# Experts by pairs of tiles with copied gate and up weights, and own places for the first eight tiles

## The chip, the core and the metric

One core of a Trainium2 chip. The metric is the device time of one execution in microseconds; the kernel before took 3332.89 us (median of three executions, 3332.68 to 3335.68).

## What is computed

Two blocks on x of shape (8, 1024, 256), each with a residual and a layer norm, all in f32:

```
x = x + LN(attn(LN(x)));  x = x + LN(ffn(LN(x)))
attn: Q, K, V of rms(x); elu on Q and K; linear attention by heads of 16:
      w = Q1 (K1' V) - lambda * Q2 (K2' V);  two rms norms; gelu MLP with W1, W2
ffn:  rms, rope, causal softmax attention with 16 query and 4 key heads, Wo; h = clip(x + .)
      flat = rms(h); probs = softmax(flat @ Wr); top 2 of 8 experts, weights normalised
      o_e = (silu(flat Wg_e) * (flat Wu_e)) Wd_e;  out = clip(h + sum_e w_e o_e)
```

Wg and Wu are (8, 256, 512), Wd is (8, 512, 256). A token takes part in two of the eight experts.

## The kernel before, in words

The 8192 tokens are 64 tiles of 128 (TT = 64, P = 128). There are three parts, one behind the other.

**`attention_kernel` (L95).** It computes everything up to the routing. Each engine's program is one list in order. A loop over periods p from -2 to 87 and over 24 slots i in each places every operation of every tile: "if i == 6 and have(p + 1): project(p + 1, False)" puts the query and key projection of tile p + 1 at slot 6 of period p. A slot fixes only the order on an engine; what really starts an operation are the waits (`need`). The causal attention ("back") is interleaved from slot 5 of period 12 on (`START`, L317), so that periods -2 to 11 hold only the front, the linear attention and the projections. The steps of the front that matter here: `x_statistics` (VectorE, L1017), `x_coefficients` (GpSimd), `normalized` (ScalarE), `transpose_x` (TensorE, L1363), `x_turned`, `project` (queries and keys into bank GA, L1408; values into bank GB, L1404), `exponentials` and `values` (ScalarE), `elu` (VectorE, L1030), `key_products` in four parts (GpSimd, L560), `sum_heads` in two halves and `turn_sums` (TensorE, L1418, L1427, bank SUM), `query_products` and `query_sums` in four parts each (VectorE, L1043, L1052). `sum_heads` of a tile waits until all four query products of the tile before have read bank SUM. `EARLY` (L320) moves the last tiles' output projection and routing forward in the list. Behind the loop the last four tiles (60 to 63) are projected and routed one by one. SyncE then loads wd, writes the last rows of h2 and writes pad rows behind each expert's rows (L479, L483). VectorE's `plan_tiles` works out the expert and the first row of every tile of the experts part. A normalised row with its routing values is scattered by GpSimd to two places of scratch_xs, sorted by expert (`scatter`, L649). At the end a block clears 123 semaphores, on all engines (L1679 to L1704).

**`run_experts` (L1719).** 136 tiles of 128 rows, in a rolled loop of eight. For each tile: SyncE loads its rows (L1765, four ahead), TensorE transposes them (`turn_x`, L1861), ScalarE evacuates (L1803), TensorE multiplies with XT stationary and the expert's gate and up weights moving, 512 columns (L1870), ScalarE applies silu (L1808), VectorE multiplies gate and up (L1831), TensorE transposes the product (L1897), ScalarE evacuates it (L1819), TensorE multiplies with wd (L1906), VectorE weights the result (L1853), and GpSimd adds it to h2 in memory by an indirect, accumulating DMA (L1790), each one behind the one before. Each f32 matmul is two records in the profile. Before a tile TensorE's sequencer reads the expert's number from memory (`value_load`, L1866). The order on TensorE in step n is:

```
gate(n+1)   transposes of AG(n)   turn_x(n+2)   up(n+1)   down(n)
```

**`finish` (L1912).** 16 groups of four tiles of h2 are loaded, clipped (GpSimd), normalised and added to x (L1937 to L2009).

A `Signal` is a semaphore with the count of its increments.

## Time and profile before

| | |
|---|---|
| median of three executions | 3332.89 us |
| the profiled execution | 3336.61 us, its span 3334.8 us |
| TensorE matmul busy | 2874.7 us (86%) |
| VectorE busy | 2155.8 us (65%) |
| GpSimd busy | 1764.0 us (53%) |
| ScalarE busy | 1671.5 us (50%) |
| mean granted TensorE clock | 0.945 |

The shares are means over stages with different limits, so they say little about one stage. PE is TensorE's matmuls, PEld its weight loads, DVE VectorE, ACT ScalarE, POOL GpSimd, SP SyncE, a q behind a name its sequencer. In a timeline a line has its start in us, its length, the engine, the line of the kernel and the operation; in brackets stands how long the engine was idle before it and what ended that.

### The profile page before, as it was taken

To read this page: it belongs to the slowest core of one execution; us is meant where nothing else is said; L and a number is where in the kernel's file an instruction comes from. 1 tells how busy PE (TensorE), PEld (TensorE's weight loads), DVE (VectorE), ACT (ScalarE), POOL (GpSimd) and SP (SyncE) were. 2 spreads that over 40 slices of the span, in tenths; PEclk is the share of its full clock that TensorE was granted. 3 is DMA by queue.
4 is the path that set the end of the run, shared out by engine and by line. 5 is a ranking of instruction groups with operands and counts; after the bars stand their busy time and mean duration, and the time that the engine had idled before them with its cause. 6 is when DMAs were issued, how large, how long until landed. Compare 5 with 4: busy or idle time off the path is not lost. (4 is left out here: it accounts for less than half of the span.)

```text
span 3334.8 us, 54048 instructions
## 1 busy us (share of the span) xinstructions
PE 2874.7 (86%) x17348; PEld 1708.5 (51%) x17349; DVE 2155.8 (65%) x4620; ACT 1671.5 (50%) x3836; POOL 1764.0 (53%) x2330
## 2 busy tenths in 40 slices
PE   3567899889989989988998997988869999999990
PEld 3344545555555555554554554444336666666660
DVE  3566887888888798789889878757522222222226
ACT  1234657657656666766765765765512222222224
POOL 5686755765775775676676576232132222222225
PEclk8777999999999999999999999999979999999995
DMA  1000000000000000000000000001243333333325
GB/s 46 0 10 10 11 9 13 14 25 13 27 20 16 29 19 19 19 22 24 12 27 22 14 25 17 14 26 58 85 125 55 58 59 57 51 59 57 57 46 205
DMA packets 102670, 123.21 MB, mean 37 GB/s; under 512 B 14384, under 2 KB 90160, under 8 KB 102448
## 3 DMA queue, kind: packets, MB, share of 16 engines
q1 hardware_dynamic: 76720, 85.54, 8.5%
q0 software_dynamic: 25728, 34.88, 6.1%
q8 instruction: 118, 1.93, 0.2%
q14 instruction: 104, 0.85, 0.1%
HBM read 58.23 MB, written 61.36 MB: 36 GB/s over the span
## 5 line engine op out<-in xcount | busy, mean ns | idle before, releaser
L897 ACT ACTIVATE wd<-SP_ 128x512 f32<-128x512 f32 (+3 forms) x1536 | 723.5, 488 | 474.1 <-PE SP_ L1576 334.4
L1194 DVE TENSOR_REDUCE NM<-MX 128x1 f32<-128x512 f32 (+3 forms) x1216 | 762.4, 654 | 244.4 <-PE MX L1533 148.3
L1530 PE MATMUL MX<-KST,QST 96*128 96x512 bf16 (+3 forms) x1536 | 454.7, 334 | 102.7 <-DVE NM L1194 91.1
L560 POOL TENSOR_TENSOR wg<-wu 128x1024 f32<-128x1024 f32 x256 | 487.7, 1925 | 103.8 <-DVE wu L1030 103.6
L1573 PE MATMUL SP_<-QST,KST 99*128 99x512 bf16 (+3 forms) x1536 | 501.7, 333 | 33.6 <-ACT wd L897 16.1
L1790 POOL DMA_INDIRECT scratch_h<-Y,XG x136 | 211.4, 1554 | 601.5 <-DVE Y L1853 504.0
L1831 DVE TENSOR_TENSOR AG<-UB,SL 128x512 f32<-128x512 f32 x136 | 94.1, 692 | 469.3 <-PE UB L1870 469.3
L1808 ACT ACTIVATE SL<-GB 128x512 f32<-128x512 f32 x136 | 81.3, 598 | 603.7 <-PE GB L1870 603.7
L1043 DVE TENSOR_TENSOR wg<-wu,SUM 128x1024 f32<-128x1024 f32 x256 | 310.2, 1212 | 101.2 <-PE SUM L1427 101.2
L1530 PEld LDWEIGHTS MX<-KST,QST 96*128 96x128 bf16 x1536 | 135.1, 98 | 431.5 <-DVE NM L1194 301.3
L1590 PE MATMUL OA<-wd,V 128*32 128x512 f32 (+3 forms) x3072 | 331.9, 504 | 0.9 <-ACT wd L897 0.4
L1052 DVE TENSOR_REDUCE wu<-wg 128x64 f32<-128x1024 f32 x256 | 307.0, 1203 | 0.3
L1418 PE MATMUL SUM<-ident,wg 128*128 128x128 f32 x2048 | 274.6, 294 | 15.1 <-DVE BR L1172 11.5
L1418 PEld LDWEIGHTS SUM<-ident,wg 128*128 128x128 f32 x2048 | 257.2, 154 | 23.8 <-DVE BR L1172 14.6
L1870 PE MATMUL GB<-wg,XTm 128*128 x544 | 258.1, 597 | 0.3 <-issue 0.3
L1906 PE MATMUL DN<-wd,AGT 128*128 x1088 | 257.1, 379 | 0.8 <-ACT AGT L1819 0.8
L1870 PE MATMUL UB<-wu,XTm 128*128 x544 | 256.8, 594 | 0.0
L1906 PEld LDWEIGHTS DN<-wd,AGT 128*128 128x128 f32 x1088 | 206.6, 190 | 86.6 <-issue 65.6
L1573 PEld LDWEIGHTS SP_<-QST,KST 99*128 99x128 bf16 x1536 | 153.7, 100 | 175.1 <-ACT wd L897 96.9
L1576 PE MATMUL SP_<-mask_kq,identb 128*128 128x128 bf16 x1024 | 224.2, 222 | 0.0
L576 POOL TENSOR_TENSOR R<-R,powers 128x16 f32<-128x16 f32 x64 | 187.1, 2924 | 5.3
L1533 PE MATMUL MX<-mask_qk,identb 128*128 128x128 bf16 (+2 forms) x704 | 174.8, 248 | 0.0
(246 smaller groups left out, 5001.3 us busy)
## 6 DMA issues: line engine op xcount, KB each, us to landing
XG<-scratch_xs SPq DMA_DIRECT2D x136, 130.0 KB, 2.1
wu<-in_L_attn_x SPq DMA_DIRECT2D x64, 128.0 KB, 2.1
scratch_x<-wu SPq DMA_DIRECT2D x64, 128.0 KB, 1.7
scratch_h<-H SPq DMA_DIRECT2D x64, 128.0 KB, 1.7
X<-scratch_x SPq DMA_DIRECT2D x16, 512.0 KB, 3.9
out<-X SPq DMA_DIRECT2D x16, 512.0 KB, 2.9
wg<-in_L_ffn_Wg SPq DMA_DIRECT2D x8, 512.0 KB, 4.3
wu<-in_L_ffn_Wu SPq DMA_DIRECT2D x8, 512.0 KB, 4.7
```

What stands on the lines that cost most here:

```text
L560: sg["prod1"].by(pool.tensor_tensor(P1[:, k // 2, (k % 2) * hh * D:(k % 2 + 1) * hh * D].rearrange("p (h e d) -> p h e d", h=hh, e=HD), QK ...
L897: sg["exp"].by(act.activation(PR[:, n % 8, q0:512], SP_[:, n % 2, q0:512], ACT.Exp))
L1043: sg["prod2"].by(dve.tensor_tensor(products(k), QK[:, t % 2, r].rearrange("p (h e) -> p h e", e=HD).unsqueeze(2).broadcast_to(shape), KVP. ...
L1052: sg["attn"].by(dve.tensor_reduce(AT[:, t % RAT, r].rearrange("p (h d) -> p h d", d=HD), products(k), AX.X, ALU.add))
L1194: sg["mx"].by(dve.tensor_reduce(NM[:, u % 2, part, i, h:h + heads], MX[:, index % 2, 0:heads * n].rearrange("p (h n) -> p h n", n=n), AX.X ...
L1418: m = pe.matmul(SUM[:, c * P:(c + 1) * P], P1[:, half, h * D + c * P:h * D + (c + 1) * P], ident[:, :], is_transpose=True, start=half == 0 ...
L1530: m = pe.matmul(out[:, k], QST[0:MROW, j % 2, g * G + h + k, i * P:(i + 1) * P], KST[0:MROW, keys % RK, g, 0:n], start=k == 0, stop=not la ...
L1573: m = pe.matmul(SP_[:, n % 2, q0:512], KST[0:KROWS, keys % RK, g, (kt % CH) * P:(kt % CH + 1) * P], QST[0:KROWS, j % 2, g * G + h, q0:512] ...
L1576: m = pe.matmul(SP_[:, n % 2, q0:q0 + P], identb[:, :], mask_kq[:, :], start=False, stop=True)
L1590: m = pe.matmul(OA[32 * h:32 * (h + 1), q0:512], V1[:, keys % RV, kt % CH, g, :], PR[:, (G * k + h) % 8, q0:512], start=kt == 0, stop=last ...
L1870: m = pe.matmul(out[:, s % 2], XT[:, s % 2, c * P:(c + 1) * P], w[:, bass.ds(e, 1), c, :].squeeze(1), start=c == 0, stop=c == FC - 1)
L1906: m = pe.matmul(DN[:, 0:D], AGT[:, s % 2, c * P:(c + 1) * P], wd[:, bass.ds(e, 1), c, :].squeeze(1), start=c == 0, stop=c == FK - 1)
```

## The change

- The experts part works on pairs of tiles, 256 rows at a time. Each expert's rows are padded to a multiple of 256, and there are 71 pairs. Now the gate and up weights are stationary and 256 columns of XT are moving, so that the product comes out transposed and its transposes (L1897) and their evacuation fall away. The stationary gate weights are first copied by ScalarE from the expert's place into a buffer WG of two (`gate_weights`), the up weights by VectorE into WU (`up_weights`). Both engines read the expert's number themselves. TX has one buffer. The loop has four pairs in a body and seven pairs behind it.
- The order on TensorE in step n is gate(n+1), down(n), up(n+1), turn_x(n+2). On ScalarE it is silu(n+1), x_evac(n+2), gate_weights(n+2). On VectorE it is the weighting of n, gate(n+1), up_weights(n+2). GpSimd scatters each pair in two halves.
- In the fill, tiles 0 to 7 have places of their own (`filled`, with the number of slots by which a step comes sooner than its old slot as the last argument). In the drain `EARLY` is 12 slots a tile instead of 6. SyncE loads six of wd's eight parts before the last rows of h2.
- Pads have 256 rows; four go through SyncE's queue and four through ScalarE's. The semaphores of the first part aren't cleared, and later parts count on from their values (`past`).
- `finish` loads two groups of four tiles with one DMA.

```
+PAIR = 2 * P
+REGION = B * S + PAIR
+
+
+UNROLL = 4
+NPAIRS = TT + E - 1
...
-        EARLY = 0, 6, 14
+        EARLY = 0, 12, 14
...
+        FILL = 8
+
+        def filled(p, i, age, slot, sooner):
+
+            return [t for t in range(p - age - 2, p - age + 4) if 0 <= t < TT
+                    and (t + age) * SLOTS + slot - (sooner if t < FILL else 0) == p * SLOTS + i]
...
+                need("h2a", LAST_CHUNK)
+                load_weight(wd, "Wd", range(1, 3))
+                need("pv", NSTEPS)
+                load_weight(wd, "Wd", range(3, 7))
                 for t in range(LAST_CHUNK, TT):
                     need("h2", t + 1)
                     sg["h2out%d" % (t % 2)].by(sp.dma_start(h2d[:, t, :], H2[:, t % 2]), 16)
-                need("pv", NSTEPS)
-                load_weight(wd, "Wd", range(3, 7))
                 need("h2a", TT)
-                load_weight(wd, "Wd", range(3))
+                load_weight(wd, "Wd", range(1))
                 need("lg", TT)
                 load_weight(wd, "Wd", range(7, E))
                 need("tables", 3)
-                sp.dma_start(dram["xs"][E * REGION:E * REGION + P], pad[:, :]).then_inc(padded, 16)
+                sp.dma_start(dram["xs"][E * REGION:E * REGION + PAIR].rearrange("(j p) f -> p j f", p=P), pads).then_inc(padded, 16)
                 need("ends", 1)
-                for e in range(E):
+                for e in range(E // 2):
...
+                    sp.dma_start(dram["xs"][bass.ds(at, PAIR), :].rearrange("(j p) f -> p j f", p=P), pads).then_inc(padded, 16)
...
-                        if i == 10 and have(p + 1):
-                            key_products(p + 1, 0)
-                        if i == 12 and have(p + 1):
-                            key_products(p + 1, 1)
-                        if i == 12 and have(p + 1):
-                            key_products(p + 1, 2)
+                        for t in filled(p, i, -1, 10, 4):
+                            key_products(t, 0)
+                        for t in filled(p, i, -1, 12, 5):
+                            key_products(t, 1)
+                        for t in filled(p, i, -1, 12, 4):
+                            key_products(t, 2)
...
-                        if i == 19 and have(p + 2):
-                            x_coefficients(p + 2)
+                        for t in filled(p, i, -2, 19, 14):
+                            x_coefficients(t)
...
+                        for t in filled(p, i, -1, 6, 6):
+                            exponentials(t)
...
+                        for t in filled(p, i, -2, 18, 11):
+                            normalized(t)
...
+                for e in range(E // 2, E):
+                    at = act.value_load(endi[0:1, e:e + 1], min_val=0, max_val=E * REGION)
+                    act.dma_start(dram["xs"][bass.ds(at, PAIR), :].rearrange("(j p) f -> p j f", p=P), pads).then_inc(padded, 16)
...
+                        for t in filled(p, i, 0, 3, 1):
+                            query_products(t, 0)
...
+                        for t in filled(p, i, -1, 9, 6):
+                            elu(t)
+                        for t in filled(p, i, 0, 9, -4):
+                            query_products(t, 2)
...
+                        for t in filled(p, i, 0, 15, 2):
+                            query_products(t, 3)
...
+                        for t in filled(p, i, 0, 0, -1):
+                            sum_heads(t, 0)
...
+                        for t in filled(p, i, -1, 6, 6):
+                            project(t, False)
+                        for t in filled(p, i, -1, 8, 5):
+                            project(t, True)
...
+                        for t in filled(p, i, -2, 20, 5):
+                            transpose_x(t)
...
-        every = [x.sem for x in sg.all] + [x.sem for x in setup.all] + loaded + stored
-        with nc.Block() as clearing:
-
-            @clearing.sync
-            def _(sp):
-                for s in every[0::5]:
-                    sp.sem_clear(s)
...
+        XG = sb("XG", [P, U, 2, ROW])
+        XT = sb("XTm", [P, 2, FC, PAIR])
+        WG = sb("WG", [P, 2, FC, F])
+        WU = sb("WU", [P, 2, FC, F])
+        SL = sb("SL", [P, 2, 2 * PAIR])
+        AG = sb("AG", [P, FK, PAIR])
+        Y = sb("Y", [P, 2, 2, D])
+        picks = sb("picks", [P, U, 2])
+        share = sb("share", [P, U, 2])
+        GB = ps("GB", [P, 2, 2 * PAIR])
+        UB = ps("UB", [P, 2, 2 * PAIR])
+        TX = ps("TX", [P, FC, PAIR])
+        DN = ps("DN", [P, 2, D])
...
+                for s in range(count):
+                    for j in range(2):
+                        pool.wait_ge(sg["y"].sem, 2 * (n0 + s) + j + 1 + CREDIT)
+                        if not (first and s == 0 and j == 0):
+                            pool.wait_ge(sg["added"].sem, (2 * (n0 + s) + j) * 16)
+                            pool.sem_inc(sg["freed"].sem, 1)
+                        pool.indirect_dma_start(
+                            out=dram["h2"], out_offset=bass.IndirectOffsetOnAxis(ap=XG[:, s % U, j, ROW - 1:ROW].bitcast(U32), axis=0),
+                            in_=Y[:, s % 2, j], in_offset=None, compute_op=ALU.add).then_inc(sg["added"].sem, 16)
...
+                act.activation(XT[:, s % 2], TX[:, :, :], ACT.Copy).then_inc(sg["xT"].sem, 1)
...
+            def silu(n):
+                for b in range(2):
+                    act.wait_ge(sg["g"].sem, 2 * n + b + 1)
+                    act.wait_ge(sg["ag"].sem, 2 * n + b - 1 + CREDIT)
+                    act.activation(SL[:, b], GB[:, b], ACT.Silu).then_inc(sg["silu"].sem, 1)
+
+            def expert(n):
+                at = texpi[0:1, n:n + 1] if isinstance(n, int) else texpi[0:1, bass.ds(n, 1)]
+                return act.value_load(at, min_val=0, max_val=E - 1)
+
+            def gate_weights(s, n):
+                e = expert(n)
+                act.activation(WG[:, s % 2], wg[:, bass.ds(e, 1)].squeeze(1), ACT.Copy).then_inc(sg["wg"].sem, 1)
+
+            act.wait_ge(wsem, 16 * 3 * E)
+            gate_weights(0, 0)
             x_evac(0, 0)
+            gate_weights(1, 1)
             x_evac(1, 1)
-            silu(0, 0)
-
-            def body(n0, i, last):
-                for s in range(U):
-                    if not (last and s + 1 >= U):
-                        silu(s + 1, n0 + s + 1)
-                    act.wait_ge(sg["tpa"].sem, n0 + s + 1 + CREDIT)
-                    act.activation(AGT[:, s % 2], TA[:, :], ACT.Copy).then_inc(sg["agT"].sem, 1)
-                    if not (last and s + 2 >= U):
+            silu(0)
+
+            def body(n0, i, count, last):
+                for s in range(count):
+                    if not (last and s + 1 >= count):
+                        silu(n0 + s + 1)
+                    if not (last and s + 2 >= count):
                         x_evac(s, n0 + s + 2)
-            act.sem_inc(sg["agT"].sem, CREDIT)
+                        gate_weights(s, n0 + s + 2)
...
+            def gate(n):
+                dve.wait_ge(sg["down"].sem, n + CREDIT)
+                for b in range(2):
+                    dve.wait_ge(sg["u"].sem, 2 * n + b + 1)
+                    dve.wait_ge(sg["silu"].sem, 2 * n + b + 1)
+                    dve.tensor_tensor(AG[:, 2 * b:2 * b + 2].rearrange("p k t -> p (k t)"), UB[:, b], SL[:, b], ALU.mult)\
+                        .then_inc(sg["ag"].sem, 1)
...
+                dve.tensor_copy(WU[:, s % 2], wu[:, bass.ds(e, 1)].squeeze(1)).then_inc(sg["wu"].sem, 1)
...
+                    for j in range(2):
+                        dve.tensor_scalar(Y[:, s % 2, j], DN[:, j], share[:, slot, j:j + 1], None, ALU.mult).then_inc(sg["y"].sem, 1)
+                    if not (last and s + 1 >= count):
+                        gate(n + 1)
+                    if not (last and s + 2 >= count):
+                        up_weights(s, n + 2)
...
+            def project(s, n, w, out, ready, done):
+                pe.wait_ge(sg[ready].sem, n + 1)
+                for b in range(2):
+                    pe.wait_ge(sg["ag"].sem, 2 * n + b - 1 + CREDIT)
+                    for k in range(2):
+                        f = 2 * b + k
+                        for c in range(FC):
+                            m = pe.matmul(out[:, b, k * PAIR:(k + 1) * PAIR], w[:, s % 2, c, f * P:(f + 1) * P],
+                                          XT[:, s % 2, c], start=c == 0, stop=c == FC - 1)
+                    m.then_inc(sg[done].sem, 1)
...
+            def combine(n, e):
+                pe.wait_ge(sg["ag"].sem, 2 * n + 2 + CREDIT)
+                pe.wait_ge(sg["y"].sem, 2 * n + CREDIT)
+                for j in range(2):
+                    for f in range(FK):
+                        m = pe.matmul(DN[:, j], AG[:, f, j * P:(j + 1) * P], wd[:, bass.ds(e, 1), f, :].squeeze(1),
+                                      start=f == 0, stop=f == FK - 1)
+                m.then_inc(sg["down"].sem, 1)
...
+            def body(n0, i, count, last):
+                for s in range(count):
                     n = n0 + s
-                    more = not (last and s + 1 >= U)
-                    e = e1
+                    more = not (last and s + 1 >= count)
+                    e = expert(n)
                     if more:
-                        e1 = expert(n + 1)
                         pe.wait_ge(sg["xT"].sem, n + 2)
-                        pe.wait_ge(sg["ag"].sem, n + CREDIT)
-                        project(s + 1, n + 1, e1, wg, GB, "g")
-                    pe.wait_ge(sg["ag"].sem, n + 1 + CREDIT)
-                    pe.wait_ge(sg["agT"].sem, n + CREDIT)
-                    for c in range(FK):
-                        m = pe.transpose(TA[:, c * P:(c + 1) * P], AG[:, s % 2, c * P:(c + 1) * P], identm[:, :])
-                    m.then_inc(sg["tpa"].sem, 1)
-                    if not (last and s + 2 >= U):
+                        project(s + 1, n + 1, WG, GB, "wg", "g")
+                    combine(n, e)
+                    if more:
+                        project(s + 1, n + 1, WU, UB, "wu", "u")
+                    if not (last and s + 2 >= count):
                         turn_x(s + 2, i)
...
+            for n in range(0, NB, 2):
+                two = halves[n // PER][:, n % PER:n % PER + 2].rearrange("p n u f -> p (n u) f")
+                sg[f"loaded{n // 2}"].by(sp.dma_start(two, hd[:, n * U:(n + 2) * U, :]), 16)
```

Some thirty further lines of the slot tables change from "if i == a and have(p + b)" to `filled` in the same way, `context` on VectorE waits for its own earlier step ("ctx"), and `plan_tiles` shifts by 8 bits instead of 7.

## Rows read from the trace of the kernel before

**Rows 1.** Windows: start:end, length, busy us of five engines; clock, DMA, GB/s.
```profile
25.00:191.00 166.00, 87.85 (x390) 67.35 (x390) 81.31 (x99) 35.57 (x85) 102.24 (x99) 0.74 0.00 1
191.00:307.00 116.00, 79.39 (x381) 58.55 (x380) 73.67 (x109) 51.16 (x111) 98.92 (x138) 0.76 0.04 12
307.00:2404.00 2097.00, 1887.55 (x13502) 1069.66 (x13502) 1723.43 (x3547) 1352.68 (x3131) 1270.42 (x1846) 0.98 0.07 23
...
2458.00:3256.00 798.00, 795.84 (x2992) 496.05 (x2992) 194.83 (x544) 186.81 (x409) 209.82 (x135) 1.00 0.32 55
```

**Rows 2.** Timeline of TensorE over one tile of the experts: start us, length, instructions.
```profile
3003.95 0.60 PE L1897 MATMUL TA<-ident,AG 128*128 128x128 f32 x4
3004.39 0.38 PE L1861 MATMUL TX<-ident,XG 128*128 128x128 f32 x2
...
3006.32 1.89 PE L1906 MATMUL DN<-wd,AGT 128*128 x8
3008.05 1.88 PE L1870 MATMUL GB<-wg,XTm 128*128 x4
3009.77 0.27 PE L1897 MATMUL TA<-ident,AG 128*128 128x128 f32 x1
```

**Rows 3.** Timeline of the last two tiles of the experts, all engines.
```profile
3252.33 0.60 PE L1897 MATMUL TA<-ident,AG 128*128 128x128 f32 x4
...
3252.97 0.60 ACT L1819 ACTIVATE AGT<-TA 128x512 f32<-128x512 f32 x1 [3.23 <-PE TA L1897]
...
3253.69 1.97 PE L1906 MATMUL DN<-wd,AGT 128*128 x8 [0.76 <-ACT AGT L1819]
3253.88 1.55 POOL L1790 DMA_INDIRECT scratch_h<-Y,XG  x1 [4.05 <-DVE Y L1853]
3255.70 0.48 DVE L1853 TENSOR_SCALAR Y<-DN,share 128x256 f32<-128x256 f32 x1 [2.31 <-PE DN L1906]
3258.23 1.55 POOL L1790 DMA_INDIRECT scratch_h<-Y,XG  x1 [2.80 <-DMA scratch_h<-Y,XG]
```

**Rows 4.** Single tile and lines, whole run: count, ns min/median/max, first, last.
```profile
L1906 PEld LDWEIGHTS DN<-wd,AGT x1088: 187/190/190, 2470.2 to 3255.1; 128*128 128x128 f32 x182
...
L1866 PEldq TENSOR_LOAD <-texpi x153: 299/496/776, 2459.5 to 3244.4; - x153
L1866 PEldq SEQ_ASSERT  x153: 18/18/18, 2460.2 to 3245.2; - x153
...
L752 ACT ACTIVATE wu<-wu x64: 621/622/630, 32.2 to 2026.2; 128x512 f32<-128x512 f32 x64
...
L769 ACT ACTIVATE SQ<-wu x64: 399/407/427, 61.5 to 2077.9; 128x256 f32<-128x256 f32 x64
```

**Rows 5.** Timeline of TensorE and of VectorE in the fill.
```profile
47.83 0.71 PE L1427 MATMUL SUM<-turn,wg 128*128 128x128 f32 x4 [0.47 <-ACT wg L758]
...
101.47 6.42 PE L1418 MATMUL SUM<-ident,wg 128*128 128x128 f32 x32
...
212.81 0.71 PE L1427 MATMUL SUM<-turn,wg 128*128 128x128 f32 x4
...
109.11 1.22 DVE L1043 TENSOR_TENSOR wg<-wu,SUM 128x1024 f32<-128x1024 f32 x1 [6.25 <-PE SUM L1427]
...
116.95 1.21 DVE L1043 TENSOR_TENSOR wg<-wu,SUM 128x1024 f32<-128x1024 f32 x1
```

**Rows 6.** Clearing block on TensorE; timeline of VectorE at the seam, GpSimd after.
```profile
L1704 PEldq EVENT_SEMAPHORE_RANGE_CLEAR  x24: 56/56/63, 2451.8 to 2454.5; - x24
...
2405.97 0.42 DVE L1236 TENSOR_TENSOR CTX<-MX,RC 128x256 f32<-128x256 f32 x1
...
2407.79 0.30 DVE L1132 MAX8 top<-LG 128x8 f32<-128x8 f32 x3
...
3267.91 1.04 POOL L1951 TENSOR_SCALAR wg<-wg 128x1024 f32<-128x1024 f32 x1 [8.12 <-DMA wg<-scratch_h]
3269.40 1.04 POOL L1951 TENSOR_SCALAR wg<-wg 128x1024 f32<-128x1024 f32 x1 [0.45 <-DMA wg<-scratch_h]
```

More of the change, by code:

```diff
@@ L66, with __init__, past @@
 class Signal:
-    def __init__(self, sem):
+    def __init__(self, sem, n=0):
         self.sem = sem
-        self.n = 0
+        self.n = n
+        self.before = n
+    def past(self, k):
+        return self.before + k
     def by(self, instruction, k=1):
@@ L1833, in _, with expert, up_weights @@
+            def expert(n):
+                at = texpi[0:1, n:n + 1] if isinstance(n, int) else texpi[0:1, bass.ds(n, 1)]
+                return dve.value_load(at, min_val=0, max_val=E - 1)
+            def up_weights(s, n):
+                e = expert(n)
+                dve.tensor_copy(WU[:, s % 2], wu[:, bass.ds(e, 1)].squeeze(1)).then_inc(sg["wu"].sem, 1)
             dve.sem_inc(sg["ag"].sem, CREDIT)
             dve.sem_inc(sg["y"].sem, CREDIT)
-            gate(0, 0)
-            def body(n0, i, last):
-                for s in range(U):
+            dve.wait_ge(wsem, 16 * 3 * E)
@@ L1844, in body @@
-                    dve.tensor_scalar(share[:, s, 0:1], first_choice, here, gain, ALU.is_equal, ALU.mult)\
-                        .then_inc(sg["picked"].sem, 1)
-                    if not (last and s + 1 >= U):
-                        gate(s + 1, n + 1)
-                    dve.wait_ge(sg["picked"].sem, n + 1)
-                    dve.tensor_tensor(share[:, s, 1:2], share[:, s, 0:1], second, ALU.add).then_inc(sg["share"].sem, 1)
-                    dve.wait_ge(sg["down"].sem, n + 1)
-                    dve.wait_ge(sg["share"].sem, n + 1)
@@ L1904, in body @@
-                    pe.wait_ge(sg["y"].sem, n + CREDIT)
-                    for c in range(FK):
-                        m = pe.matmul(DN[:, 0:D], AGT[:, s % 2, c * P:(c + 1) * P], wd[:, bass.ds(e, 1), c, :].squeeze(1),
-                                      start=c == 0, stop=c == FK - 1)
-                    m.then_inc(sg["down"].sem, 1)
+                        project(s + 1, n + 1, WG, GB, "wg", "g")
+                    combine(n, e)
+                    if more:
+                        project(s + 1, n + 1, WU, UB, "wu", "u")
@@ L1968, in norm @@
             def norm(n):
[L1969 removed]
+                act.wait_ge(sg["shift"].sem, sg["shift"].past(n + 1))
                 for u in range(U):
```

371 lines of the change are left out of this document (155 added, 216 removed).

## The prediction

> **What bounds the kernel now.** I read the busy time by stage first [rows 1]. There are four stages: the fill up to about 307 us, attention and routing up to 2404 us, the experts from 2458 to 3256 us, and the last layer norm. In the experts TensorE is busy for 795.8 of 798 us at a granted clock of 1.00. All other engines are busy for less than 211 us there, so this stage is as long as TensorE's program. In the fill nobody is full: TensorE 53%, VectorE 49%, GpSimd 62% up to 191 us, then 85% on GpSimd up to 307 us. Between them TensorE is busy 90% at clock 0.98.
>
> Then the timeline of one tile of the experts [rows 2]. Eight matmul records with 256 moving columns start every 1.72 to 1.73 us (3006.32 to 3008.05), four transposes 0.44 us apart from the next group. A tile takes 5.82 us (3003.95 to 3009.77).
>
> **The experts, new.** A pair of tiles is 48 records of 256 columns: 16 each for gate, up and down. Six groups at 1.725 us are 10.35 us. The four transposes of x add 0.44 us. The eight transposes of AG per pair are gone. If TensorE never waited, a pair would take 10.79 us where two tiles take 11.64; but there are 71 pairs instead of 68, so the most to be had is 791.5 (136 x 5.82) less 766 = 25 us.
>
> TensorE does wait, and this is the term that decides. Before, the transposes of tile n+2 stand ahead of the up projection and the down matmuls, so ScalarE's evacuation has over 3 us of cover. After, `turn_x(s + 2)` is the last thing in a step, and the next step begins with a wait for that very XT and with the gate projection of that very pair. That projection also waits for signal wg, and ScalarE makes that copy only *after* the evacuation of the same pair (`x_evac`, then `gate_weights`). So in each step TensorE idles through: last transposes, evacuation, read of the expert number, copy of 128x1024, semaphore.
>
> The price. The drain of the old stage shows the first half of this chain in the same shapes [rows 3]: four transposes start at 3252.33, ScalarE begins at 3252.97 (0.64 later), evacuates 128x512 in 0.60, and TensorE's next matmul starts at 3253.69, 0.12 after the end. Its group of eight ends 0.08 to 0.09 late because nothing was prefetched. The read of the expert number isn't shown on ScalarE. On TensorE's sequencer it takes 0.7 to 0.8 us from the load to the assert [rows 4]. It can start when the evacuation is dispatched. Lower end: fully under the evacuation, copy starts 0.60 after it; upper end 1.1, the longest load of 0.78 with its register work. I take 0.85, the nearest row plus an address computation. A copy of 1024 columns isn't shown either; 256 columns take 0.41 and 512 take 0.62 from SBUF [rows 4], so 0.21 for each 256, and 1.04 us for 1024. From the start of the transposes to the next matmul: 0.64 + 0.85 + 1.04 + 0.12 = 2.65 us; 0.44 of it is the transposes themselves, and 0.09 is the unprefetched start. Stall: 2.30 us (2.05 to 2.55).
>
> A pair then takes 10.79 + 2.30 = 13.09 us. The first two pairs are prepared ahead (2 x 2.74 less), and the last down projection waits 1.0 us for its gate product, which I set against the rounding of the start. Start and end otherwise cost as before. 71 x 13.09 - 5.5 - 791.5 = **+132 us** (+115 to +149).
>
> What hides the rest of a pair. GpSimd's two scatters wait for one another: where a scatter waited only for the one before, issues stood 4.35 us apart (3253.88 to 3258.23 [rows 3]), 8.7 us for two against 13; uncovered it would be nothing up to 13 us. VectorE's copy of the up weights stands behind the gate products and is wanted a whole down projection later. VectorE's weighting of Y, SyncE's loads two pairs ahead (freed by scatters of two pairs before) and TensorE's own number read lie inside 13 us as well. Behind TensorE's new wait stand everything it issues, hence VectorE and GpSimd; nothing runs past it.
>
> On the weight loads: a load for 128 columns takes 0.190 us [rows 4] and eight records still start 0.216 us apart [rows 2], so loads hide behind 256 columns. The Trainium skill ("TensorE: Matmul & The Clock Gate", Part 3, what overlaps) says that a weight load overlaps matmuls in flight only when the row group differs. By that rule the loads, of which a pair has 48, would stand beside the matmuls. The trace disagrees for this very shape, and I keep 0.216.
>
> **The fill.** Eight tiles go from turned sums at 47.83 to 212.81 [rows 5], 20.6 us each. The ring is: sum of heads and turned sums (7.64 us, 101.47 to 109.11), VectorE's products and sums (the fourth product ends at 118.16), and meanwhile projection, exponential, ELU and GpSimd's key products of the next tile, which in the old order start only after the turned sums. The new places put the next tile's gate to this ring early: x statistics, normalising, transposes and the query/key projection before the sum of heads. What is left is the SUM bank's own ring: 7.64, 0.3 for the value projection that now lies in it, four products, ELU, head norm and two sums on VectorE (9.05 less one sum of about 1.1), 0.1 for the semaphore: 16.0 us. GpSimd needs about 14. Five tiles at 16.0, one at 18 with the hidden layer's matmuls, one at 18.8 where the second layer's output must leave the bank first, one at 20.5 in the old order: 137 against 165, **-28 us**. Ends: -12 if only half of the slack goes, -45 if TensorE, idle less, keeps its full clock. Periods 8 to 12 I leave at nothing, since GpSimd is 85% busy there [rows 1].
>
> **The seam and the end.** The clearing block goes: TensorE's 24 clears run from 2451.8 to 2454.5 with barriers around them [rows 6], **-3.1**. Routing of tile 59 moves before the end of attention: its choice begins at 2407.79 though the context is done at 2406.39 [rows 6], **-1.4** (0 to -4). Pads: twice the rows per pad, on two queues; GpSimd's last scatters hide them, and without that cover they would cost some 3 us. The order of the wd loads is nothing while they land before the first projection. The first x load is twice as big: **+1.0** (0 to 2). The last pair has two scatters in a row behind the last down projection, 4.35 us where 2.53 of waiting (3255.70 to 3258.23) stood, plus Y: **+3.2** with the hand-over. The first load of the last stage is doubled; the first clip starts at 3267.91 and loads of 512 KB followed at some 1.5 us: **+1.5**. The rest of that stage is bound by its chain, and fewer issues are nothing.
>
> Sum: 132 - 28 - 3.1 - 1.4 + 1.0 + 3.2 + 1.5 = +105. The profiled execution took 3336.6 us, 3.7 over the median of 3332.9: 3441.8 in its terms, **3438 us** as a median.
>
> **The rivals.**
> - *Only the evacuation is waited for* (0.07): the copy of gate weights is somehow in time, so the stall is 0.64 + 0.60 + 0.12 - 0.44 + 0.09 = 1.01 us. For it: the shape in [rows 3] shows just that. Against it: the order of ScalarE's program. 69 x 1.29 = 89 us less: 3349 us.
> - *The other side: no stall* (0.05): TensorE runs through, because x and weights of pair n+2 are there when the up projection of n+1 ends. It decides at a hand-over hidden by at least 2.2 of the 2.30 us. Then 69 x 2.30 = 159 less: 3279 us, faster. The code's order is against it.
> - *The clock falls* (0.08): with TensorE 82% busy in bursts. At 90% busy it was 0.98 [rows 1], at 53% 0.74. At 0.9 in the experts each pair's 10.79 grows by 1.2 us: +85, 3523 us.
> - *Weight loads stop hiding* (0.02) where 512 moving columns were: 32 x 0.19 x 71 = +432, 3870 us. The page's sentence above is this rival; [rows 2] show the contrary.
> - *The new places bring nothing* (0.04): 3466 us, inside the range.
>
> **How the numbers follow.** The forecast has 0.74. Its ends, stall -17 to +17, fill -17 to +16, the small terms 6 each way, give 3398 to 3477; with the case of the fill I say 3395 to 3478 for 8 in 10. This kernel's measurement can tell about 0.2% (7 us) from no change. Faster: the no-stall rival, 0.05. Same 0.01. Slower 0.94.
>
> **What would show it.** In the timeline of a pair, TensorE should idle some 2.3 us before the gate projection, released by ScalarE's WG copy, not by XTm; ScalarE's chain evacuation, copy should end there. Turned sums should come every 16 us for tiles 1 to 5 and the attention stage should start some 28 us earlier. Down matmuls should still start 0.216 us apart. Wrong would be: a gap that XTm ends, a clock below 0.97 in the experts, scatters that TensorE waits for, or a fill as long as before.

## The result, and the profile after

| | before | after |
|---|---|---|
| median | 3333.64 us (4 executions) | 3467.59 us (4 executions, 3464.98 to 3469.08) |
| ratio, 95% interval | | 1.040, 1.038 to 1.042 |
| profiled execution / span | 3336.61 / 3334.8 us | 3468.11 / 3466.2 us |
| TensorE matmul busy | 2874.7 us (86%) | 2897.5 us (84%) |
| mean granted clock | 0.945 | 0.942 |

The changed kernel is 134 us slower, in the direction and inside the range of the forecast (+105). In the changed kernel L1901 is the gate and up projection, L1910 the down projection, L1887 the transposes of x, L1800 their evacuation, L1814 and L1848 the copies of the gate and up weights, L1873 the weighting of Y, L1786 the scatter, L1448 the turned sums.

First the windows by stage of the changed kernel, with the columns of [rows 1]: length, busy us of five engines, clock, DMA share, GB/s.

```profile
25.00:165.00 140.00, 92.05 (x416) 62.61 (x417) 91.36 (x114) 41.56 (x97) 117.53 (x117) 0.81 0.01 2
165.00:262.00 97.00, 69.61 (x353) 51.49 (x352) 65.05 (x94) 46.33 (x98) 84.30 (x121) 0.78 0.04 13
262.00:2361.00 2099.00, 1890.42 (x13446) 1071.70 (x13446) 1723.41 (x3547) 1347.57 (x3118) 1274.10 (x1849) 0.97 0.07 24
2410.00:3385.00 975.00, 814.18 (x3692) 697.35 (x3692) 247.09 (x568) 203.53 (x285) 221.09 (x142) 0.96 0.27 48
```

The last row answers to the last of [rows 1]. TensorE is busy 814 us, 18 more than before, and from its first transposes to the last Y the stage became 165 us longer (962.7 instead of 797.7 us). The window is 12 us wider than that stretch; inside the stretch TensorE now idles 148.5 us, where it was full before. The fill (the first two rows) is 45 us shorter, at a clock of 0.81 where it was 0.74.

How the difference builds up along the two spans:

| event | before | after | shift |
|---|---|---|---|
| turned sums of tile 12 | 306.92 | 262.14 | -44.8 |
| last turned attention output (L1571; before: L1550) | 2404.52 | 2371.23 | -33.3 |
| first transposes of x of the experts | 2458.00 | 2418.35 | -39.7 |
| last Y of the experts | 3255.70 | 3381.04 | +125.3 |
| first load of the last stage | 3263.90 | 3393.87 | +130.0 |
| end of the span | 3334.8 | 3466.2 | +131.4 |

So the experts part alone lost 165 us. Its timeline, first TensorE over two pairs, then ScalarE over the first of them (start, length, instruction; in brackets the idle time before it and what ended that):

```profile
3000.92 3.71 PE L1901 MATMUL GB<-XTm,WG 128*128 128x256 f32 x16 [2.07 <-ACT WG L1814]
3004.47 3.62 PE L1910 MATMUL DN<-wd,AG 128*128 x16
3007.92 3.62 PE L1901 MATMUL UB<-XTm,WU 128*128 128x256 f32 x16
3011.38 0.60 PE L1887 MATMUL TX<-ident,XG 128*128 128x128 f32 x4
3014.02 5.40 PE L1901 MATMUL GB<-XTm,WG 128*128 128x256 f32 x16 [2.04 <-ACT WG L1814]
3019.26 3.62 PE L1910 MATMUL DN<-wd,AG 128*128 x16
...
3012.01 0.60 ACT L1800 ACTIVATE XTm<-TX 128x512 f32<-128x512 f32 x1 [6.75 <-PE TX L1887]
3012.73 1.06 ACT L1814 ACTIVATE WG<-wg 128x1024 f32 x1
```

This is the stall that the forecast described, by its own two instructions: transposes at 3011.38, evacuation at 3012.01, copy from 3012.73 to 3013.79, next matmul at 3014.02, released by WG. The group of the gate projection on the profile's page of the changed kernel gives the sum (busy us, mean ns | idle us before it and what ended most of it):

```profile
L1901 PE MATMUL GB<-XTm,WG 128*128 128x256 f32 x1136 | 291.5, 414 | 146.9 <-ACT WG L1814 135.8
```

The rows above hold a second thing that the forecast did not have in its sum. The gate projection at 3014.02 took 5.40 us for the same 16 records that took 3.71 at 3000.92. Two windows of the changed kernel, inside that projection and in the down and up projections behind it:

```profile
3014.80:3017.20 2.40, 2.40 (x7) 1.93 (x6) 0.00 (x0) 0.00 (x0) 1.41 (x1) 0.50 0.00 0
3020.00:3023.00 3.00, 3.00 (x16) 2.64 (x15) 0.00 (x0) 0.06 (x1) 0.00 (x0) 1.00 0.00 0
```

The granted clock is 0.50, the lower of the two levels (1.2 GHz), inside the projection that follows the gap, and 1.00 (2.4 GHz) again in the down and up projections behind it. From one gate projection to the next the kernel takes 12.86 to 13.40 us, 13.18 in the mean (52 pairs), but 14.78 to 15.04, 14.89 in the mean, in 16 pairs, every third to fifth.

The Trainium skill ("TensorE: Matmul & The Clock Gate", Part 1, the second HAM failure mode) describes this in a bf16 kernel that cycles through its PSUM banks: TensorE idles a little between groups of matmuls, often enough that the clock swings between its two levels. This trace agrees, for an f32 kernel with gaps of 2.0 to 2.3 us in the pairs of its rolled loop.

### The profile page after: what moved, and what is told of

Its sections match the earlier page's. It is cut to its first block and busy times, and to the rows that moved or that the text cites. A ratio compares the mean times of both kernels' runs of the same rounds, so it can differ in the third digit from the quotient of the medians.

```text
span 3466.2 us, 54343 instructions
## 1 busy us (share of the span) xinstructions
PE 2897.5 (84%) x18048; PEld 1902.4 (55%) x18049; DVE 2206.7 (64%) x4645; ACT 1689.1 (49%) x3713; POOL 1774.8 (51%) x2336
## 5 line engine op out<-in xcount | busy, mean ns | idle before, releaser
L1786 POOL DMA_INDIRECT scratch_h<-Y,XG x142 | 221.7, 1561 | 756.4 <-DVE Y L1873 486.2
L1873 DVE TENSOR_SCALAR Y<-DN,share 128x256 f32<-128x256 f32 x142 | 62.2, 480 | 566.2 <-PE DN L1910 566.2
L1901 PE MATMUL GB<-XTm,WG 128*128 128x256 f32 x1136 | 291.5, 414 | 146.9 <-ACT WG L1814 135.8
L1901 PEld LDWEIGHTS GB<-XTm,WG 128*128 128x128 f32 x1136 | 229.8, 207 | 197.0 <-issue 162.8
L1800 ACT ACTIVATE XTm<-TX 128x512 f32<-128x512 f32 x71 | 42.4, 597 | 468.9 <-PE TX L1887 468.8
L1439 PEld LDWEIGHTS SUM<-ident,wg 128*128 128x128 f32 x2048 | 248.3, 150 | 38.0 <-DVE BR L1191 14.4
L1910 PE MATMUL DN<-wd,AG 128*128 x1136 | 256.9, 379 | 0.9 <-DVE AG L1839 0.9
L1901 PE MATMUL UB<-XTm,WU 128*128 128x256 f32 x1136 | 256.8, 379 | 0.0
L1910 PEld LDWEIGHTS DN<-wd,AG 128*128 128x128 f32 x1136 | 215.8, 190 | 30.6 <-issue 1.3
L1901 PEld LDWEIGHTS UB<-XTm,WU 128*128 128x128 f32 x1136 | 215.8, 190 | 29.3
```

What stands on the lines that cost most here:

```text
L1439: m = pe.matmul(SUM[:, c * P:(c + 1) * P], P1[:, half, h * D + c * P:h * D + (c + 1) * P], ident[:, :], is_transpose=True, start=half == 0 ...
L1901: m = pe.matmul(out[:, b, k * PAIR:(k + 1) * PAIR], w[:, s % 2, c, f * P:(f + 1) * P], XT[:, s % 2, c], start=c == 0, stop=c == FC - 1)
L1910: m = pe.matmul(DN[:, j], AG[:, f, j * P:(j + 1) * P], wd[:, bass.ds(e, 1), f, :].squeeze(1), start=f == 0, stop=f == FK - 1)
```

## The experiments

Ten kernels. All but e8 start from the changed kernel. A ratio is to the kernel before, run beside it, with its 95% interval. That kernel's median was 3333.4 us beside e1 to e4, 3335.4 beside e6 to e9 and 3337.9 beside e5 and e10, so differences of medians across these three sets are uncertain by some 2 to 4 us. Each trace is of one execution, and the executions of one program lie 2 to 7 us apart (13 us in e1).

**e1: the copy ahead of the evacuation.** ScalarE copies the weights of pair n+2 before it evacuates that pair's transposes.

```diff
-                        x_evac(s, n0 + s + 2)
                         gate_weights(s, n0 + s + 2)
+                        x_evac(s, n0 + s + 2)
```

> ScalarE copies the gate weights of pair n+2 before it evacuates x of that pair; the rest is the changed kernel. Theory (TensorE waits for evacuation, number read and copy in a row): only the evacuation is left, so the idle time before each gate projection falls from 2.05 to 2.3 us to about 1.0, a pair takes about 11.8 us, and with the shorter gap the clock is no longer at half in every fourth pair: 69 x 1.2 = 83 us and some 25 us of slow matmuls less, 3360 us. Rival (the evacuation alone or the semaphores are the wait): nothing moves, 3467 us. If the clock falls are not tied to the length of the gap, 3385 us.

Measured: 3343.10 us, ratio 1.003 (1.002 to 1.005). TensorE and ScalarE in the steady state of e1:

```profile
3001.19 0.60 PE L1887 MATMUL TX<-ident,XG 128*128 128x128 f32 x4
3002.55 3.72 PE L1901 MATMUL GB<-XTm,WG 128*128 128x256 f32 x16 [0.77 <-ACT XTm L1800]
...
3001.82 0.60 ACT L1800 ACTIVATE XTm<-TX 128x512 f32<-128x512 f32 x1 [5.46 <-PE TX L1887]
...
3007.11 1.06 ACT L1814 ACTIVATE WG<-wg 128x1024 f32 x1 [0.21 <-issue]
```

Two swapped lines are worth 124 us. The gap is 0.77 us and XTm ends it; the copy lies under the down projection. A pair takes 11.83 us, and behind the first none is at the lower clock. The 3360 us that were expected took the gap at 1.0 us and had no gain ahead of the experts. The parts: 69 x (13.18 - 11.83) = 93, 16 pairs x 1.70 = 27 for the clock, and 5.5 that the attention part ended sooner (below): 125. The forecast's rival "only the evacuation is waited for" is this kernel, and its stall of 1.01 us is the 11.83 - 10.80 = 1.03 measured here. But its total of 3349 was put on the forecast's own fill and clock.

**e2: the turn ahead of the up projection.** Now TensorE has 3.45 us of other work between the transposes and the wait for them.

```diff
                     combine(n, e)
+                    if not (last and s + 2 >= count):
+                        turn_x(s + 2, i)
                     if more:
                         project(s + 1, n + 1, WU, UB, "wu", "u")
-                    if not (last and s + 2 >= count):
-                        turn_x(s + 2, i)
```

> TensorE transposes x of pair n+2 before the up projection of n+1 and not behind it; the rest is the changed kernel. Theory: evacuation and copy (2.4 us) fit under the up projection (3.4 us), TensorE does not wait, a pair takes 10.8 us, the granted clock is 1.00: 69 x 2.3 = 159 us and some 25 us of half clock less, about 3280 us, faster than the kernel before. Rival: the two scatters of a pair (2 x 4.35 us and up to 5.5 each) or the gate product become the wait, so that a pair takes 11.3 to 11.8 us, 3320 to 3350 us.

Measured: 3271.62 us, ratio 0.982 (0.980 to 0.984). This is the best version of the study: 62 us faster than the kernel before. The timeline of TensorE and ScalarE in e2, and in a second block the gate projection's group on its page:

```profile
3003.25 0.60 PE L1887 MATMUL TX<-ident,XG 128*128 128x128 f32 x4
3003.68 3.62 PE L1901 MATMUL UB<-XTm,WU 128*128 128x256 f32 x16
3007.14 3.62 PE L1901 MATMUL GB<-XTm,WG 128*128 128x256 f32 x16
...
3003.88 0.60 ACT L1800 ACTIVATE XTm<-TX 128x512 f32<-128x512 f32 x1 [3.29 <-PE TX L1887]
3004.60 1.06 ACT L1814 ACTIVATE WG<-wg 128x1024 f32 x1
```

```profile
L1901 PE MATMUL GB<-XTm,WG 128*128 128x256 f32 x1136 | 258.4, 381 | 0.0
```

The chain on ScalarE is as long as in the changed kernel; it ends at 3005.66 and is wanted at 3007.14. TensorE waits for nothing and a pair takes 10.80 us, every one behind the first at the full clock. 69 x (13.18 - 10.80) = 164, 27 for the clock and 5 for the attention part make 196; measured 196. So nothing else in the changed experts costs time, the scatters included: in e2 GpSimd's two scatters of a pair stand 4.4 to 6.5 us apart, and TensorE waits for neither.

**e3: no own places for the first eight tiles.**

```diff
-        FILL = 8
+        FILL = 0
```

> The first eight tiles get their old places back; the rest is the changed kernel. If the new places are what brings the start of attention forward by 44.8 us, then 3467 + 45 = 3512 us; if a part of it comes from elsewhere in the change, less.

Measured: 3506.11 us, ratio 1.052 (1.050 to 1.054), 38.5 us slower than the changed kernel. The turned sums of tile 12 come at 307.03, as before the change, and the attention part ends at 2404.59 (before: 2404.52), although this kernel still pulls the last tiles' routing forward by 12 places. The new places are the whole of what the attention part gained. At the experts' first transposes 33.8 us of it are left (2452.18 against 2418.35). The other 5 us of the 38.5 arise in the experts themselves, which took 967.9 us here and 962.7 in the changed kernel, with two more gate projections at the lower clock and gaps of 2.15 us instead of 2.13; the edit doesn't touch them, so this is no price of the places.

**e4: the routing pulled forward by 6 places, as before.**

```diff
-        EARLY = 0, 12, 14
+        EARLY = 0, 6, 14
```

> The last tiles of the routing are moved forward by 6 slots a tile as before, and not by 12; the rest is the changed kernel. The changed kernel lost 8 us of its lead between 2235 us and the end of attention at 2371 us and won 2 behind it. Theory A (the 12 slots do this): this kernel ends about 6 us earlier, 3461 us. Theory B (the loads of wd or the clock's state do it): no change, 3467 us.

Measured: 3461.29 us, ratio 1.039 (1.037 to 1.041). Six us less, which looks like theory A. The same edit on e2 does not repeat it.

**e5: the same edit on e2.**

> The version with the turn ahead of the up projection, and the routing of the last tiles pulled forward by 6 places a tile instead of 12. Theory A (as with the changed kernel, the pull of 12 delays the tiles behind it a little and brings nothing): 3 to 6 us less than with 12, 3266 to 3269 us. Rival B (the pull of 12 made the experts start sooner): 3272 or more.

Measured: 3272.07 us, ratio 0.981 (0.979 to 0.982), against 3271.62 (0.982) with 12 places. No gain can be told here; but the kernel before was 4.5 us slower beside e5 than beside e2, so a gain of 3 to 6 us isn't excluded by the times. The traces say more. From the start of the 56th to the start of the last of the 64 groups of L1571 (or of its counterpart in e8) it takes 177.2 to 177.3 us with 6 places, in e4, e5 and e8. With 12 it takes 177.5 to 178.2 in e1, e2 and e10, but 180.9 to 181.5 in the changed kernel, e6, e7 and e9. From there to TensorE's last routing matmuls it takes 27.4 us with 6 places and 25.5 to 26.5 with 12. So the pull of 12 delays the tiles behind it, as theory A has it, by 0.3 to 4.3 us, and wins 1 to 2 us back: up to the experts' first transposes e2 is 1.2 us better with it than e5, and the changed kernel 2.9 us worse than e4. Why the delay differs among programs with the same edit is open.

The rest of e4's gain lies further ahead, where the edit moves nothing. The last of these groups starts at 2371.23, 2372.33 and 2371.67 in the changed kernel, e6 and e7, and between 2365.65 and 2366.40 in e1, e2, e9 and e10 (2365.59 in e5, 2362.89 in e4), though apart from e4 and e5 the attention part of all of them is the same to the instruction. The 5.5 us gather gradually along the stage (0.5 to 1.6 us by 603 us, 3 to 4.5 by 1812). I did not find their cause. With one trace of each, it is not shown that the program and not the execution decides it, though e7's median, 8 us above e2's, holds more than its edit explains. So totals of two programs are only comparable to some 6 us here, and below that I go by stretches of the trace.

**e6: half the copy.** The copy of 69 pairs moves 512 columns; their products use the rest of an older expert's weights.

```diff
-                act.activation(WG[:, s % 2], wg[:, bass.ds(e, 1)].squeeze(1), ACT.Copy).then_inc(sg["wg"].sem, 1)
+                w = wg[:, bass.ds(e, 1)].squeeze(1)
+                if isinstance(n, int):
+                    act.activation(WG[:, s % 2], w, ACT.Copy).then_inc(sg["wg"].sem, 1)
+                else:
+                    act.activation(WG[:, s % 2, :1], w[:, :1], ACT.Copy).then_inc(sg["wg"].sem, 1)
```

> ScalarE's copy of the gate weights moves only the first half (512 of 1,024 columns) for 69 of the 71 pairs; the other half keeps what an earlier pair left, so the expert products of those pairs are of mixed weights. Theory A (the copy stands in the chain that TensorE waits for, and the clock falls come from how long TensorE is idle): the copy shrinks from 1.06 to some 0.6 us, which takes 69 x 0.47 = 32 us away, and with a gap of 1.6 us instead of 2.1 the clock falls (some 26 us in all) get fewer or vanish: 3409 to 3435 us, 3409 if they all go. Rival B (the gap is not the copy's but another wait's, which steps in as soon as the copy is short): within 5 us of 3467. Rival C (the clock falls have nothing to do with the gap): 3435, with as many pairs at the low clock as before.

Measured: 3419.22 us, ratio 1.025 (1.023 to 1.026). The copy takes 0.63 us instead of 1.06, the gap 1.75 instead of 2.13 in the mean: 69 x 0.38 = 26 us. Two pairs instead of 16 are at the lower clock: some 24 us more. Sum 50, measured 48. Theory A: the copy stands in the chain, and with shorter gaps the clock falls less often. The gaps are uneven here, 1.62 to 2.08 us in the rolled loop; the two pairs at the lower clock had 1.87 and 1.88.

**e9: the copy without the read of the expert's number.** The copy of 69 pairs takes expert 0's weights, so its address is fixed. The products are then of another expert's weights.

```diff
-                e = expert(n)
-                act.activation(WG[:, s % 2], wg[:, bass.ds(e, 1)].squeeze(1), ACT.Copy).then_inc(sg["wg"].sem, 1)
+                w = wg[:, bass.ds(expert(n), 1)].squeeze(1) if isinstance(n, int) else wg[:, 0]
+                act.activation(WG[:, s % 2], w, ACT.Copy).then_inc(sg["wg"].sem, 1)
```

> ScalarE copies the gate weights of expert 0 for 69 of the 71 pairs and so does not read the pair's expert number into a register; the length of the copy is the same. My forecast gave this read 0.12 us in the gap of each pair. Theory A (the read stands between the evacuation and the copy): 69 x 0.12 to 0.46 us less, 3436 to 3459 us. Rival B (the read is done while the evacuation still runs, so the copy follows it as soon as it would without): within 5 us of 3467.

Measured: 3415.91 us, ratio 1.024 (1.023 to 1.026), below both theories. TensorE and ScalarE in e9:

```profile
2911.36 0.60 PE L1887 MATMUL TX<-ident,XG 128*128 128x128 f32 x4
2913.78 1.56 PE L1901 MATMUL GB<-XTm,WG 128*128 128x256 f32 x6 [1.82 <-ACT WG L1814]
...
2912.00 0.60 ACT L1800 ACTIVATE XTm<-TX 128x512 f32<-128x512 f32 x1 [6.75 <-PE TX L1887]
2912.49 1.05 ACT L1814 ACTIVATE WG<-wg 128x1024 f32<-128x1024 f32 x1
```

The copy starts 0.49 us behind the start of the evacuation, where it was 0.72 and more. The gap falls from 2.13 to 1.82 us, so the read, with the address made from it, costs 0.31 us in each pair, 21 us in all. (The expectation names 0.12 us as the forecast's price of the read; by the forecast's own terms it was 0.85 - 0.60 = 0.25.) It also made the gap uneven (2.04 to 2.34 in the rolled loop); now it is 1.81 to 1.83. And behind the first no pair is at the lower clock any more, another 27 us. With 5 us of the attention part that is 53, measured 52. Both theories had left the clock out.

**e10: e9 with the copy in two halves.** A small dose the other way: the gap longer again, but even.

```diff
-                act.activation(WG[:, s % 2], w, ACT.Copy).then_inc(sg["wg"].sem, 1)
+                act.activation(WG[:, s % 2, :1], w[:, :1], ACT.Copy)
+                act.activation(WG[:, s % 2, 1:], w[:, 1:], ACT.Copy).then_inc(sg["wg"].sem, 1)
```

> As the run without the read of the expert number (3416 us, gap 1.82 us in every pair, no clock fall), but the copy is made in two halves, which took 0.63 us each. The gap should be 0.2 us longer, about 2.05 us, the length of the shortest gaps of the changed kernel, and the same in every pair. Theory A (the clock falls come with gaps of that length): 3416 + 14 = 3430 us and up to 26 us for the falls, 3440 to 3456. Rival B (they come from something else in the changed kernel, the read or its uneven length): 3430 us, and every pair at the full clock.

Measured: 3466.25 us, ratio 1.039 (1.037 to 1.040), 50 us slower than e9. TensorE over two pairs of e10, and in a second block the window inside the first projection:

```profile
2800.48 0.60 PE L1888 MATMUL TX<-ident,XG 128*128 128x128 f32 x4
2803.00 5.40 PE L1902 MATMUL GB<-XTm,WG 128*128 128x256 f32 x16 [1.92 <-ACT WG L1815]
...
2815.14 0.60 PE L1888 MATMUL TX<-ident,XG 128*128 128x128 f32 x4
2817.65 3.71 PE L1902 MATMUL GB<-XTm,WG 128*128 128x256 f32 x16 [1.91 <-ACT WG L1815]
```

```profile
2803.80:2806.20 2.40, 2.40 (x7) 1.87 (x6) 0.00 (x0) 0.00 (x0) 1.39 (x1) 0.50 0.23 14
```

The gap grew by 0.09 us, from 1.82 to 1.91, where 0.2 was expected, and 27 pairs instead of none are at the lower clock: 14.65 us each, 1.68 more than the other pairs' 12.97. 27 x 1.68 = 45, and 0.09 x 69 = 6 for the gap itself: 51. That is more than theory A allowed, which had counted on 16 such pairs. So neither the read nor an uneven gap is needed for the clock to fall, and rival B fell. Between e9 and e10 three things differ: the gap is 0.09 us longer, so is the pair, and the copy is two instructions. That the length of the gap is what matters is the likely reading, with e1, e6 and e9 beside it, but no run separates the three. How often the clock falls does not simply grow with the gap, either: the changed kernel has longer gaps (2.13) and only 16 such pairs. Nor does the gap's length tell which pair is hit. In e10 the gaps ahead of the 27 slow projections are 1.91 us long like the others, and in the changed kernel those ahead of the 16 are 2.04 to 2.29 us, 2.17 in the mean, against 2.12 for the rest. What decides it I leave open.

**e8: the kernel before, with the new places alone.** The fill edits of the change on the old kernel: the old experts, clearing block and routing.

> The kernel before with only the places of the first eight tiles changed; experts by single tiles, clearing block and routing places as before. Theory A (the new places give the whole of what the attention part gained, 33 to 45 us, and nothing eats it later): 3334 - 40 = 3294 us, between 3288 and 3301. Rival B (my forecast's 28 us): 3306. Rival C (what the first tiles gain is given back before the experts start, because a later transfer sets that start): within 5 us of 3334.

Measured: 3293.87 us, ratio 0.987 (0.986 to 0.989). The places are worth 41 to 43 us by themselves: 41.5 by the medians, 43 by the ratio, 40.8 in the traces. The turned sums of tile 12 come at 262.62, the experts' first transposes at 2417.19 and the end at 3294.0: 44.3, 40.8 and 40.8 us sooner. The experts stage is unchanged:

```profile
2417.00:3214.00 797.00, 795.13 (x2991) 495.99 (x2992) 194.62 (x543) 186.82 (x409) 209.59 (x135) 1.00 0.32 55
```

**e7: e2 with the clearing block back between the parts.** It clears 103 semaphores, one fifth of them on each engine.

```diff
+        every = [x.sem for x in sg.all] + [x.sem for x in setup.all]
+        with nc.Block() as clearing:
+
+            @clearing.sync
+            def _(sp):
+                for s in every[0::5]:
+                    sp.sem_clear(s)
...
```

> The version with the turn of a pair's tokens placed ahead of the up projection (3271.6 us), with the block that clears the 103 semaphores put back between the parts. Theory A (the block stands on the path): the stretch from TensorE's last routing turn to the first turn of the experts is 2.6 to 3.1 us longer, 3274 to 3275 us. Rival B (another wait, the loads' or the scatters' end, covers it): the stretch is unchanged.

Measured: 3279.68 us, ratio 0.983 (0.982 to 0.985). The stretch from TensorE's last routing matmuls to its first transposes in e7 and, below the dots, in e2:

```profile
2398.17 0.61 PE L1532 MATMUL SUM<-BR,ones 128*128 128x32 f32 x2
2421.40 1.11 PE L1915 MATMUL TX<-ident,XG 128*128 128x128 f32 x4 [22.61 <-DMA XG<-scratch_xs]
```

```profile
2392.18 0.61 PE L1532 MATMUL SUM<-BR,ones 128*128 128x32 f32 x2
2412.73 1.12 PE L1887 MATMUL TX<-ident,XG 128*128 128x128 f32 x4 [19.94 <-DMA XG<-scratch_xs]
```

23.23 against 20.55 us: the block stands on the path and costs 2.7 us (it clears 103 semaphores; the block of the kernel before cleared 123). The rest of the 8 us lies ahead of this stretch and is the difference told at e5.

## Why the prediction was right, and where not

**The experts: right, and the term that decided.** The forecast said a stall of 2.30 us a pair by ScalarE's chain, a pair of 13.09 us and +132 us; measured 13.18 and +165 with the clock. Its floor of 10.79 us is e2's 10.80. The pieces: 0.64 from transposes to evacuation (0.63), 0.85 from evacuation to copy (0.49 and 0.31 for the read, so 0.80), 1.04 for the copy, drawn from copies of 256 and 512 columns (1.06), and 0.12 to the next matmul (0.23, from 3013.79 to 3014.02; mine was too small). 71 pairs x 0.09 = 6 us is what these errors come to.

**The clock: a term the sum did not have.** The step that failed is "a pair then takes 10.79 + 2.30": it added an idle time to a work time at clock 1.00. The forecast had the falling clock as a rival with 0.9 for the stage and +85 us. It came in a mild form: 16 of some 70 pairs at the lower level in their gate projection, 0.96 over the stage (below the 0.97 that the forecast named as a sign of being wrong), 16 x 1.70 = 27 us. 132 + 6 + 27 = 165, which is the shift of the experts. I had given it 0.08 as an either-or. The rows pointed that way: the clock was 0.74 and 0.76 in the stages with gaps [rows 1].

**The fill: right in its mechanism, 17 us too small.** Predicted -28, measured -44.8 in the profiles, and 41 to 43 in a whole kernel (e8); e3's 38.5 holds 5 us that arise elsewhere. The timeline of the changed kernel for two tiles:

```profile
79.39 1.91 PE L1439 MATMUL SUM<-ident,wg 128*128 128x128 f32 x16
82.61 1.97 PE L1439 MATMUL SUM<-ident,wg 128*128 128x128 f32 x16 [1.31 <-POOL wg L574]
85.28 0.61 PE L1448 MATMUL SUM<-turn,wg 128*128 128x128 f32 x4
94.74 4.35 PE L1439 MATMUL SUM<-ident,wg 128*128 128x128 f32 x32
99.80 0.61 PE L1448 MATMUL SUM<-turn,wg 128*128 128x128 f32 x4
...
91.38 2.34 DVE L1062 TENSOR_TENSOR wg<-wu,SUM 128x1024 f32<-128x1024 f32 x2
...
100.44 1.22 DVE L1062 TENSOR_TENSOR wg<-wu,SUM 128x1024 f32<-128x1024 f32 x1 [3.56 <-PE SUM L1448]
```

It is the ring that the forecast named: the fourth product ends at 93.72, the sum of heads starts 1.0 us later, and the next products 5.70 us after that. Tiles 1 to 5 come every 13.0 to 14.5 us, not 16.0. The mis-sized term is the 7.64 us from sum of heads to products: it was taken from a tile of the old fill [rows 5], where the 32 matmuls took 6.42 us at a clock of 0.56. Windows over these 32 matmuls, of the kernel before:

```profile
101.40:107.90 6.50, 6.49 (x34) 6.25 (x32) 0.42 (x1) 0.69 (x2) 5.30 (x6) 0.56 0.00 0
```

and of the changed kernel:

```profile
94.70:99.20 4.50, 4.50 (x35) 4.29 (x34) 2.15 (x5) 1.09 (x3) 4.25 (x7) 0.87 0.00 0
```

TensorE idles less and is granted 0.87, so the link takes 5.70 us. The forecast's end of -45 said just this and was not taken. The periods up to the turned sums of tile 8 sum to 127.4 us, where 137 was said and 165.0 stood before. The other 7 us are an earlier first tile (43.74 instead of 47.83) and 3 us in tiles 8 to 12, which I had left at nothing.

**The seam.** From the end of attention to the first transposes it took 47.1 us instead of 53.5, so -6.4 where -3.1 - 1.4 + 1.0 = -3.5 was said. From the end of attention to the last routing matmuls it is 26.3 us instead of 28.4, -2.2 where the forecast had -1.4 for the earlier routing, though the pull of 12 takes that back ahead of this stretch (e5). From there to the issue of the first x load it is 18.0 us instead of 22.9: -5.0, of which the clearing block is -2.7 by e7 (-3.1 said); the other 2.3 the forecast did not have, and no run here separates them. From that issue to the first transposes it is 2.9 us instead of 2.1: +0.8 for the larger load (+1.0 said). Between tile 12 and the end of attention 11.5 us of the fill's gain were lost in the changed kernel, which the forecast had at nothing. 4.3 of them were lost in e8 too (44.3 to 40.0), with 6 places; of the other 7.2, 3.6 lie behind the 56th group of L1571 (e5) and the rest further ahead, unexplained.

**Tail and last stage.** Here are the last scatters, the last stage's first load and its first clip in the changed kernel, beside [rows 3] and [rows 6]:

```profile
3381.04 0.88 DVE L1873 TENSOR_SCALAR Y<-DN,share 128x256 f32<-128x256 f32 x2 [3.34 <-PE DN L1910]
3383.21 1.56 POOL L1786 DMA_INDIRECT scratch_h<-Y,XG  x1 [2.74 <-DMA scratch_h<-Y,XG]
3387.59 1.56 POOL L1786 DMA_INDIRECT scratch_h<-Y,XG  x1 [2.82 <-issue]
3393.87 2.36 SPq L1969 DMA_DIRECT2D wg<-scratch_h  x4
...
3399.37 1.04 POOL L1980 TENSOR_SCALAR wg<-wg 128x1024 f32<-128x1024 f32 x1 [10.21 <-DMA wg<-scratch_h]
```

From the last Y to the load it takes 12.8 us instead of 8.2: +4.6, where +3.2 was said. The two scatters stand 4.38 us apart (4.35 said), but the first still waits for the one before it, so the last issue is 6.55 us behind Y where it was 2.53: +4.0. The load then comes 6.28 us behind it instead of 5.67: +0.6. The clip comes 5.5 us after the load instead of 4.0 (+1.5 said), and the end of the span shifts by 1.4 more.

**The weight loads.** The rival with exposed loads did not come. e2 has 48 loads and 48 matmul records of 256 columns in a pair of 10.80 us, four transposes included, so no load adds anything. The Trainium skill ("TensorE: Matmul & The Clock Gate", Part 3) lets a load overlap only when the row group differs; these all use the full array, and the trace disagrees with it again.

The total: +33 in the experts, -17 in the fill, some +11 given back along the attention part, -3 in the seam, +1 in the tail against what was said: +25 to +26. The spans differ by 131.4, the sum said 105. That the total lies inside the range owes something to luck: the misses of one sign alone, 33 in the experts, 11 along the attention part and 1 in the tail, would have given 3438 + 45 = 3483 us, above the upper end of 3478.

## What to carry to other kernels

Where an engine's program ends a step with the producer of what its next step begins with, count every hand-over between them, and look one order further: here the copy stood behind the evacuation for no reason (124 us), and moving the transposes one projection ahead hid the whole chain (196 us) without touching any work. A price for idle time on TensorE is only a lower end if the gaps repeat, because the clock can fall with them: e10, with gaps only 0.09 us longer than e9's, took 50 us more, and in the fill, where TensorE idled less, the 32 matmuls between sum of heads and products took 4.35 us instead of 6.42. And a slot table of a pipeline's fill is worth a look of its own: some 41 us of this kernel came from eight tiles of 64.

## What was not expected of the hardware

- The clock's answer to short gaps is sharp. With 1.82 us of idle time in each pair of 12.87 us no pair behind the first ran at the lower level (e9); with 1.91 in 12.97 it was 27 (e10); with 2.13 in the mean and 13.18 it was 16 (the changed kernel); with 1.75 and uneven, 2 (e6); with 0.77 in 11.83, none (e1).
- Without a read of its address ahead of it, ScalarE's copy starts 0.49 us behind the start of the evacuation before it; with the read it was 0.80 in the mean. Without it, the copy's row starts 0.11 us before the evacuation's row ends (2912.49 against 2912.60 in e9).
- Programs with the same attention part, instruction for instruction, end it in two groups 5.5 us apart, by one trace of each. A whole-kernel difference of this size says nothing here unless the trace shows its place.
